# Last attention projection with residual and two norms: products taken tile by tile, a third rounded unit in a buffer of its own, the second norm's scaling on ScalarE

## The reference

```python
x_attn = x_attn @ W_proj + b_proj          # 625 x 768, W_proj 768 x 768
y = x + x_attn
mu = jnp.mean(y, axis=-1, keepdims=True)
var = jnp.mean(jnp.square(y - mu), axis=-1, keepdims=True)
return (y - mu) * jax.lax.rsqrt(var + LN_EPS) * gamma + beta
...
x = x + _L3_gnn_ref(...) + _L3_mix_ref(xn[None], ...)[0]
x = x + _L3_ffn_ref(_layernorm(x, axis=-1)[None], L3_ffn_Wg, L3_ffn_W1, L3_ffn_W2)[0]
```

## Time and profile before

| what | value |
|---|---|
| median of the runs | 3058.88 us (3057.87 to 3059.01) |
| the profiled execution: time, span of the core | 3053.72 us, 3051.9 us |
| busy share of the span: TensorE, VectorE, ScalarE, GpSimd | 90%, 48%, 37%, 23% |
| mean granted TensorE clock, as a share of full | 0.963 |

### The profile page before, as it was taken

How to read it: one execution, slowest core, us unless ns; L and a number is a source line. 1 busy time by engine, 2 the same in 40 slices (tenths; PEclk the granted TensorE clock), 3 DMA queues, 4 the chain that set the end, 5 groups by cost and what they waited for, 6 DMA issues and landing times. The chain is left out here.

```text
span 3051.9 us, 48899 instructions
## 1 busy us (share of the span) xinstructions
PE 2755.0 (90%) x20123; PEld 2495.1 (82%) x20123; DVE 1454.8 (48%) x3675; ACT 1119.0 (37%) x2073; POOL 705.6 (23%) x260
## 2 busy tenths in 40 slices
PE   8999999996779999998999999899887899997697
PEld 8999999993349878987979899896566888794697
DVE  8877575572130335477624422416746455005542
ACT  6632265540013114258312533324424243444131
POOL 0143311110002412311343333233013241102121
PEclk9999999998889999999999999999998999999799
DMA  2022221108952112220212122221001121100121
GB/s 67 15 85 64 81 68 37 68 18 349 416 221 63 60 30 63 73 73 12 69 41 64 62 80 76 63 64 36 1 16 43 52 79 47 45 22 12 32 63 57
DMA packets 163791, 220.39 MB, mean 72 GB/s; under 512 B 21521, under 2 KB 142795, under 8 KB 163570
## 3 DMA queue, kind: packets, MB, share of 16 engines
q1 hardware_dynamic: 163570, 217.26, 21.3%
HBM read 215.31 MB, written 1.92 MB: 71 GB/s over the span
## 5 line engine op out<-in xcount | busy, mean ns | idle before, releaser
L58 PE MATMUL ps<-weights_r,buf_r 128*125 128x256 f32 (+3 forms) x4080 | 548.9, 286 | 23.4 <-POOL weights_r L268 8.3
L58 PEld LDWEIGHTS ps<-weights_r,buf_r 128*125 128x125 f32 (+1 forms) x4080 | 517.2, 188 | 27.6 <-issue 14.6
L268 POOL TENSOR_TENSOR weights_r<-weights,head_weights_r 128x1536 fp32r<-128x1536 f32 (+1 forms) x78 | 274.2, 3516 | 1115.0 <-ACT head_weights_r L261 1115.0
L268 POOL TENSOR_TENSOR weights_r<-weights,weights_r 128x1536 fp32r<-128x1536 f32 (+1 forms) x79 | 273.4, 3461 | 1081.0 <-ACT weights_r L261 1081.0
L58 PE MATMUL ps<-xT_r,weights_r 128*128 128x376 f32 (+1 forms) x2100 | 345.6, 310 | 0.0
L58 PE MATMUL ps<-head_weights_r,buf_r 128*125 128x256 f32 (+2 forms) x2400 | 329.1, 283 | 0.0
L58 PEld LDWEIGHTS ps<-xT_r,weights_r 128*128 128x128 f32 x2100 | 314.3, 189 | 4.2 <-issue 1.7
L58 PEld LDWEIGHTS ps<-head_weights_r,buf_r 128*125 128x125 f32 x2400 | 305.4, 187 | 0.0
L58 PE MATMUL ps<-weights_r,xT_r 128*125 128x256 f32 x1680 | 232.5, 282 | 10.4 <-DVE buf_r L714 8.7
L261 ACT ACTIVATE head_weights_r<-weights 128x1536 fp32r<-128x1536 f32 (+1 forms) x78 | 114.3, 1466 | 332.5 <-PE ps L58 207.7
L58 PEld LDWEIGHTS ps<-weights_r,xT_r 128*125 128x125 f32 x1680 | 212.9, 186 | 12.3 <-issue 9.3
(11 more groups left out here) (358 smaller groups left out, 4356.3 us busy)
## 6 DMA issues: line engine op xcount, KB each, us to landing
expert_regions<-in_L_ffn_w SPq DMA_DIRECT2D x64, 576.0 KB, 14.8
expert_regions<-in_L_ffn_w SPq DMA_DIRECT2D x48, 768.0 KB, 20.5
weights<-in_L_mix_fc_w SPq DMA_DIRECT2D x24, 768.0 KB, 4.5
weights<-in_L_gnn_W SPq DMA_DIRECT2D x18, 768.0 KB, 4.6
weights<-in_L_ffn_W SPq DMA_DIRECT2D x12, 768.0 KB, 4.6
weights<-in_L_mix_w_mapT SPq DMA_DIRECT2D x9, 768.0 KB, 5.0
weights<-in_L_gnn_W_out SPq DMA_DIRECT2D x9, 768.0 KB, 4.6
weights<-in_L_mix_kqv_wT SPq DMA_DIRECT2D x9, 768.0 KB, 4.6
```

The costliest lines, as they stand in the source:

```text
L58: mm = net.nc.tensor.matmul(ps, net.r(stationary(s, k)), net.r(moving(m, k)), start=(n == 0 and k == 0), stop=(stop and n == 2 and k == kc ...
L268: self.nc.gpsimd.tensor_tensor(self.r(load.dst), load.dst, self.r(load.high), ALU.subtract).then_inc(self.low_made, 1)
```

## The change

The products are taken tile by tile: the three units of tile t follow one another on TensorE, and turn(t-1) stands between the second and the third. VectorE takes the three pairs of add and moments of a tile, with inverse2 and a new entry `shift` for tile t-1 after the first pair, and low(t-1) after mean(t). `shift` computes -mean2 * rstd2, and `norm` becomes an ACTIVATE on ScalarE with scale rstd2 and bias shift, ahead of the highs of its tile. Since all three units are now in use at once, the third unit's high part goes into `G[3]`, free from the stage's start (`split_into`), and is made first thing in the stage on ScalarE and GpSimd; the router's weights and the first expert's unit are split at the end of ScalarE's list. The slots of the first two units are free after the products NT * n + NT - 1, which now stand near the end of the list.

```diff
--- before.py
+++ after.py
@@ -236,6 +236,13 @@
 
         return bass.AP(self.rounded[ap.tensor.name], ap.offset, ap.ap)
 
+    def split_into(self, load, high, free):
+
+        p, c, w = load.dst.shape
+        load.unit = len(self.units)
+        load.high, load.high_free, load.segment = high[:p, 0:c * w].rearrange("p (c w) -> p c w", c=c), free, self.segment
+        self.units.append(load)
+
     def split(self, load):
 
         p, c, w = load.dst.shape
@@ -1068,33 +1075,33 @@
 
 
 
-    def __init__(self, net, xT, units, y, gamma, x, out, outT, eps, after=None, tiles=None):
+    def __init__(self, net, xT, units, y, gamma, x, out, outT, eps, high, free, after=None, tiles=None):
         Stage.__init__(self, net, after)
         self.xT, self.units, self.tiles, self.y, self.gamma, self.x, self.out, self.outT, self.eps = xT, units, tiles, y, gamma, x, out, outT, eps
         self.columns, self.loads = None, [gamma]
         self.rstd, self.rstd2 = net.st[:TP, 70:75], net.st[:TP, 191:196]
         self.mv2 = net.st[:TP, 560:570].rearrange("p (t s) -> p t s", t=NT)
+        self.shift = net.st[:TP, 186:191]
         self.last = NT * (len(units) - 1)
         self.order = {e: [] for e in ("pe", "act", "dve")}
         pe, act, dve = (self.order[e] for e in ("pe", "act", "dve"))
-        for i in range(NT * len(units)):
-            t = i - self.last
-            pe.append(("product", i))
-            dve += [("add", i), ("moments", i)]
-            if t < 0:
-                continue
+        for t in range(NT):
+            for n in range(len(units)):
+                pe.append(("product", NT * n + t))
+                if n == 1 and t > 0:
+                    pe += [("turn", t - 1, g) for g in range(2)]
+                dve += [("add", NT * n + t), ("moments", NT * n + t)]
+                if n == 0 and t > 0:
+                    dve += [("inverse2", t - 1), ("shift", t - 1)]
+                    act += [("norm", t - 1)] + [("high", t - 1, g) for g in range(2)]
             dve.append(("mean", t))
             if t > 0:
-                dve += [("inverse2", t - 1), ("norm", t - 1)]
+                dve += [("low", t - 1, g) for g in range(2)]
             dve += [("inverse", t), ("scaled", t), ("sum", t), ("stats", t, 0), ("stats", t, 1), ("mean2", t)]
             act += [("root", t), ("root2", t)]
-            if t > 0:
-                act += [("high", t - 1, g) for g in range(2)]
-            if t > 1:
-                dve += [("low", t - 2, g) for g in range(2)]
-        dve += [("inverse2", NT - 1), ("norm", NT - 1)] + [("low", t, g) for t in (NT - 2, NT - 1) for g in range(2)]
-        act += [("high", NT - 1, g) for g in range(2)]
-        pe += [("turn", t, g) for t in range(NT) for g in range(2)]
+        dve += [("inverse2", NT - 1), ("shift", NT - 1)] + [("low", NT - 1, g) for g in range(2)]
+        act += [("norm", NT - 1)] + [("high", NT - 1, g) for g in range(2)]
+        pe += [("turn", NT - 1, g) for g in range(2)]
         bases = dict(pe=net.pe.planned, act=net.act.planned, dve=net.dve.planned)
         self.at = {e: {q: bases[e] + i + 1 for i, q in enumerate(seq)} for e, seq in self.order.items()}
         self.bank = {}
@@ -1104,18 +1111,30 @@
         self.made = [(net.dve.sem, self.at["dve"]["low", t, 1]) for t in range(NT)]
         self.take(**{e: len(seq) for e, seq in self.order.items()})
         for n, u in enumerate(units):
-            u["load"].used, u["load"].used_at = [(net.pe.sem, self.p0 + NT * (n + 1))], (len(net.stages) - 1, n)
-        self.weights = list(dict.fromkeys(u["load"] for u in units))
-        for load in self.weights:
+            u["load"].used, u["load"].used_at = [(net.pe.sem, self.at["pe"]["product", NT * n + NT - 1])], (len(net.stages) - 1, n)
+        self.weights = [u["load"] for u in units]
+        for load in self.weights[:-1]:
             net.split(load)
+        net.split_into(self.weights[-1], high, free)
 
     def tensor(self, pe):
         if self.tiles is None:
             self.begin(pe)
-        for i in range(NT * len(self.units)):
-            self.product(pe, i, self.bank["product", i])
-        for t in range(NT):
-            self.turn(pe, t)
+        for q in self.order["pe"]:
+            if q[0] == "product":
+                self.product(pe, q[1], self.bank[q])
+            else:
+                self.turn(pe, *q[1:])
+
+    def turn(self, pe, t, g):
+
+        b = self.bank["turn", t, g]
+        if b >= BANKS:
+            pe.wait_ge(*self.free(b))
+        self.wait(pe, "act", "norm", t)
+        for c in range(3):
+            mm = self.nc.tensor.transpose(self.net.ps[:, b % BANKS, c * TP:(c + 1) * TP], self.out[:, t, (3 * g + c) * 128:(3 * g + c + 1) * 128], self.net.ident[:TP, :TP])
+        mm.then_inc(self.net.pe.sem, self.net.pe.one())
 
     def place(self, t, g):
 
@@ -1158,9 +1177,9 @@
             elif kind == "inverse2":
                 self.wait(dve, "act", "root2", t)
                 ins = nc.vector.reciprocal(col(self.rstd2, t), col(self.rstd2, t))
-            elif kind == "norm":
+            elif kind == "shift":
                 dve.wait_ge(done.sem, done.issued)
-                ins = nc.vector.tensor_scalar(self.out[:, t], self.x[:, t], self.mv2[:, t, 0:1], col(self.rstd2, t), ALU.subtract, ALU.mult)
+                ins = nc.vector.tensor_scalar(col(self.shift, t), self.mv2[:, t, 0:1], col(self.rstd2, t), -1.0, ALU.mult, ALU.mult)
             else:
                 hi, lo, ps = self.place(t, q[2])
                 self.wait(dve, "act", "high", t, q[2])
@@ -1170,8 +1189,7 @@
     def scalar(self, act):
         self.begin(act)
         nc, done, eps = self.nc, self.net.act, self.net.eps[self.eps][:TP, :]
-        for load in self.weights[:-1]:
-            self.net.split_high(load.unit + 2, load.segment)
+        self.net.split_high(self.weights[-1].unit, self.weights[-1].segment)
         for q in self.order["act"]:
             kind, t = q[:2]
             if kind == "root":
@@ -1180,13 +1198,21 @@
             elif kind == "root2":
                 self.wait(act, "dve", "mean2", t)
                 ins = nc.scalar.activation(self.rstd2[:, t:t + 1], self.mv2[:, t, 1:2], ACT.Sqrt, bias=eps)
+            elif kind == "norm":
+                self.wait(act, "dve", "shift", t)
+                ins = nc.scalar.activation(self.out[:, t], self.x[:, t], ACT.Identity, bias=self.shift[:, t:t + 1], scale=self.rstd2[:, t:t + 1])
             else:
                 hi, lo, ps = self.place(t, q[2])
                 self.wait(act, "pe", "turn", t, q[2])
                 ins = nc.scalar.activation(hi, ps, ACT.Identity)
             ins.then_inc(done.sem, done.one())
-        for load in self.weights[-1:]:
+        for load in self.weights[1:]:
             self.net.split_high(load.unit + 2, load.segment)
+
+    def gpsimd(self, pool):
+        self.net.split_low(self.weights[-1].unit, self.weights[-1].segment)
+        for load in self.weights[1:]:
+            self.net.split_low(load.unit + 2, load.segment)
 
 
 class LinearReluNorm(LinearNorm):
@@ -3631,7 +3657,7 @@
     QueryApply(net, stacks, net.fw[:, 0:512], [feat(b, 4) for b in (G[2], G[4])], kv, net.fn, pair(net.XT, G[1]), 1e-6, net.lnc[:, 1:2])
     XT = pair(net.XT, G[1])
     units = linear_units(net, ins["L3_mix_W_proj"], tok(G[5]), "add", tok(G[5]))
-    normed = LinearResidualNorm(net, XT, units, tok(G[5]), net.row(ins["L3_mix_gamma"]), R, tok(G[0]), XT, 1e-5, now() + bias_out.ends() + shift.ends())
+    normed = LinearResidualNorm(net, XT, units, tok(G[5]), net.row(ins["L3_mix_gamma"]), R, tok(G[0]), XT, 1e-5, G[3], now(), now() + bias_out.ends() + shift.ends())
     start = now()
     router(net, XT, ins["L3_ffn_Wg"], logits, tiles=normed.made)
     TopTwo(net, logits, gates, "top", sel, first)
```

## The result

The changed kernel takes 3069.59 us (median), the kernel before 3057.47 beside it: the ratio is 1.004, with a 95% interval of 1.0027 to 1.0053, so it is slower, by 12.1 us between the medians. Forecast were 14.9 us more, 3073.8 us, from a kernel before at 3058.88; of the 4.2 us between that and the measured time 1.4 are the kernel before, which ran that much faster here, and 2.8 the change. The profiled execution's span grew from 3051.9 to 3066.4 us.

A forecast was written before the change was run, and what follows sets the result against it. TensorE bound the stage's first 33.4 us, VectorE the next 21.7. A later router start of 5.8 us, 8.4 of half clock in the rounds and 0.7 in the router sum to 14.9: 3073.8 us, range 3064.5 to 3077.5.

The forecast's parts named there:

- to the end of the third product: Start of the stage on TensorE: the third product ends at 2828.65, with nothing counted for a wait.
- four rounds at full clock: From the first tile's third product to the last's: 10.43 us, then three rounds of 10.85.
- half clock in the rounds: TensorE's clock falls in idle stretches of 3.6 us before four turns, costing 2.1 us each, 8.4 in all.
- tail, last third product to router: From the last third product's end through statistics, norm, turns, highs and weight rounding to the router's first matmul: 10.06 us.
- router slower: Router's matmuls on TensorE: 0.4 to 1.4 us more from half clock after a pause; 0.7 taken.
- The ring: turn(t-1) before tile t's third product waits for tile t-1's whole statistics chain and norm: 10.85 us a round.
- Third unit: Its rounding on ScalarE and GpSimd is ready by 2825.7, its product starts at 2826.3: no wait counted.
- Router's weights: Rounded behind the last high: ScalarE 0.24, GpSimd 0.28, hand-offs 0.15 us, new on the path to the router.
- The first: Rival: VectorE's work of 7.5 us a tile sets the round, not the ring; 3052.5 us; chance 0.05.
- The second: Rival: the clock doesn't fall in the gaps or costs nothing there; 3064.7 to 3065.4 us; chance 0.10.
- the ScalarE rule: Additions and multiplications belong on VectorE: the norm there would save 0.66 us per ring and tail, 3.3 in all.
- Signs: Marks expected in the new trace, such as TensorE idle 3.5 us before four turns and third products 10.5 us apart.

The follow-up runs named there:

- x2_warm: Changed kernel with 22 added matmuls of 256 columns, results overwritten, ahead of the turns of each of tiles 0 to 3; 3063.01 us, ratio 1.0019.
- x5_router_early: Changed kernel with the high part of the router's weights made on ScalarE ahead of its last norm, not behind its last high; 3069.14 us, ratio 1.0038.
- x3_norm_vector: Changed kernel with the second norm's scaling back on VectorE in the place of the shift, without ScalarE's norm; 3060.92 us, ratio 1.0015.

## Why the prediction was right

The mechanism and the direction held: the turns held the third products, and the clock fell in the gaps. By the steps of the sum:

| term | forecast | measured |
|---|---|---|
| to the end of the third product | 0 | +0.7 |
| four rounds at full clock | 43.0 | 41.8 (`x2_warm`) |
| half clock in the rounds | 8.4 | 6.6 |
| tail, last third product to router | 10.06 | 9.89 |
| router slower | 0.7 | 1.4 |
| router's end, later by | 14.9 | 13.3 |
| total | 14.9 | 12.1 (medians), 14.5 (spans) |

The forecast of 14.9 comes closer to the router's 13.3 than its terms do. The ring (1.1) and the half clock (1.8) were taken too long, and against them stand 0.7 of router taken too short and 0.7 at the stage's start that the change didn't cause. That they cancel in part is chance.

- **The ring.** The round was forecast at 10.85 us and is 10.56. Two terms were 0.11 to 0.16 too long: inverse2 starts 0.75 us after the addition ahead of it instead of 0.91 (2847.54 to 2848.29 above), and six transposes take 0.59 before the next matmul starts, not 0.70 (2861.90 to 2862.49). The norm was exact, 1.03 us, from the two-operand price; the shift took 0.21, where 0.27 was taken.
- **The clock.** It fell in all four gaps. The cost of 2.1 us a round was the least certain term; 1.66 was measured, near the lower of the two values (1.55), as in three of four gaps half clock was over after 3.4 us (1.3 to 1.5 a round). In the first it lasted 6.8 us, and that round lost 2.4.
- **Third unit.** Its low part was ready at 2822.51 + 3.47 = 2825.98, and its product started near 2827.37, behind the second unit's, 1.4 us later: no wait, as counted. That the third product ended 0.7 us late is the clock, which stayed half for 4.6 us after the stage's start against 3.1 before. It is no effect of the change: in the other traces with the products tile by tile this mark lies between 8.03 and 9.17 us.
- **Router's weights.** The pause of 1.07 us was there and released by GpSimd, and its removal gave the start back (`x5_router_early`). That it also cost clock in the router was sized at half of what it was: 7.91 us against 6.49 before.
- **The rivals.** The first, VectorE's work as the pace at 7.5 us, gave 3052.5 for the router 6.4 us earlier. It was wrong for this kernel and right for the one with the turns moved: rounds of 7.6 to 7.8, 3049.55, 7.3 us under a kernel before at 3056.88. The second, a clock that stays up, gave 3065, 6 us more than before; `x2_warm`, which is that case by force, took 3063.01, 6 us more than 3056.88. On the ScalarE rule: 0.66 us a round and in the tail was the price, 0.53 and 0.60 were measured, 2.7 of the 3.3 us. The other 2.7 us of the 5.4 in the stage are the clock, which fell in two gaps only (`x3_norm_vector`).
- **Signs.** Most of those named came: the turns released by ScalarE's norm, third products 11.9 to 12.6 us apart, norm 1.03, the router released by GpSimd. Two were missed by a little. TensorE was to idle 3.5 us or more before each turn and idled 3.0 to 3.4, since the round is shorter by 0.3 and half clock reaches into the next tile's first product; and the router was to start 10 us or more after the last product and started after 9.9.
- Left over are 2.4 us between the span's growth and the medians' difference. The executions spread by several us, so nothing is built on it.

The page "ScalarE: Activation LUTs" of the Trainium skill, "Rules for kernel authors", says to use VectorE and not ScalarE for additions and multiplications, of which the norm's scaling is made. The traces agree for the one instruction (0.68 against 1.03 us) and for the closed ring, and not for the open one, where VectorE sets the pace. The Trainium skill's page "TensorE: Matmul & The Clock Gate", "Step-by-step: what each phase is for", states that matmuls keep their order; the trace agrees, as no product ran ahead of a waiting turn.

## What to carry to other kernels

Equal totals of work per tile say nothing of the pace when one engine's list puts a step that depends on the whole chain of tile t-1 ahead of a product that starts the chain of tile t: add up the ring of waits, and let the dependent step stand behind the product. Whether a step is better on another engine depends on which bound holds: take its latency inside a ring, its busy time where an engine is the pace. And idle stretches of 2.4 to 3.4 us in front of TensorE's work can be paid a second time by the clock, here 6.6 of the 20 us that the order cost.

## What was not expected of the hardware

The length of an idle stretch of some 3 us doesn't tell whether the clock falls. In `x3_norm_vector` it fell with 2.39 and 2.80 us and not with 2.81 and 2.79; in the changed kernel's trace it fell in all four gaps (2.98 to 3.40 us), and in the first gap of `x5_router_early` it didn't:

```profile
2840.18 0.83 PE L1136 MATMUL ps<-ident,buf 125*128 125x125 f32 x6 [2.99 <-ACT buf L1205]
2840.77 0.95 PE L58 MATMUL ps<-weights_r,xT_r 128*125 128x256 f32 x6
2841.57 0.88 PE L58 MATMUL ps<-buf_r 128*125 128x256 f32 x6
```

It can fall after work has resumed: the third turn of the changed kernel ran at full clock (0.83 us), and half clock began 1.2 us after its start, at 2863.1, and met the third product.
